# Seam between a ConvNeXt block's first convolution and its MLP: statistics of four images ahead, tiles three ahead, dummy TensorE passes

## The chip, the core and the metric

One Trainium2 chip, of which the kernel uses one core (TensorE, VectorE, ScalarE, GpSimd, and SyncE as a queue of transfers). The metric is the time of one execution on the device in microseconds (us), the median of several runs. In the profile the engines are called PE (TensorE), PEld (its weight loads), DVE (VectorE), ACT (ScalarE), POOL (GpSimd) and SP (SyncE).

## What is computed

x has 16 images of 96 channels of 56 x 56 points, in float32. Cut to what matters:

```python
y = depthwise_conv_7x7(x, dw_w) + dw_b                  # per channel
mu, var = mean_c(y), var_c(y)                           # over the 96 channels of a point
y = (y - mu) * rsqrt(var + 1e-6) * ln_w + ln_b
y = gelu(y @ w1 + b1)                                   # 96 -> 384
gx = sqrt(sum_over_points(y ** 2))                      # per image and hidden channel
nx = gx / (mean_hidden(gx) + 1e-6)
y = grn_gamma * (y * nx) + grn_beta + y
z = x + y @ w2 + b2                                     # 384 -> 96
out = depthwise_conv_3x3(floor_to_fixed(z), round_pow2(w)) + floor_to_fixed(bias)
```

## The kernel before, in words

Three stages follow each other, each with an instruction stream per engine that is written out by hand and tied by semaphores (`wait_ge`, `then_inc`; `need` is a wait that is dropped where its value is zero). No scheduler reorders anything: what an engine does next is what stands next in its block.

**First stage (7x7 convolution).** 96 channels in 24 batches of four (`CB`), all 16 images at once. PE turns rows (`tin`, L636), multiplies by banded tables (L664) and turns the result back (`back`, L686). ACT copies the results out (`yt_copy`, L803, and `out_copy`, L810), SP stores the convolved channels to `y_scratch` (L366). DVE keeps a running mean over the channels, and the running sum of squared deviations (`update`, L1017: the deviation L1021, the mean L1023, the weighted square L1025), POOL adds the squares up (`m2`, L557). In these arrays a column stands for points of one of the 16 images.

**Seam.** After channel 95: DVE makes the variance (L1031), ACT its root (L870, a table load and one pass), DVE the reciprocal with one Newton step (L1043 to L1047) and copies it into image order (`in_order`, L1038 to L1040). PE turns it to rows (L724, eight transposes), DVE copies the rows to SBUF (L1051), ACT stores them to `stats_scratch` (L872), waits until they have landed, and loads them back repeated over 96 partitions into `rb`: the first tile of image 0 (L876), the other six tiles of image 0 as one transfer (L877), image 1 (L878). SP first stores the tables of the last stage (`lines_c`, L407 to L409), waits for its stores, loads image 0 of y whole (L472), waits for `r_in[0]` (that is L877) and then loads image 1 of y whole, then seven tiles of x, and then images from 2 on by tiles (L478, L479).

**MLP.** An image is 7 tiles (`NCH`) of 448 points. For tile t of image i: DVE multiplies y by the factor of each point (`scale`, L1065) and rounds to the matmul's format (`high`, L1070), POOL makes the remainder (`low`, L568), PE multiplies by w1 in three parts and three groups of 128 hidden channels (`up`, L733 to L735: 9 matmuls), ACT applies gelu (L893). The squares of the hidden values are summed by ACT (L860), and of image 0 mostly by DVE (L1084); `part` 0 is the first four tiles, `part` 1 the last three, and m the group of hidden channels. Then DVE, POOL, PE and DVE make the GRN factors (`grn_sums` L1092, L577, the matmul with ones L758, `grn_scale` L1098 to L1109) that scale w2. PE's `down` (L743) multiplies by w2; ACT prepares x plus a constant (`with_constant`, L867), DVE adds and floors (L1117 to L1137), SP stores z (L488). The `steps` go over images: in step i, PE interleaves `up` of image i with `down` of image i-1, which runs `LEAD` = 2 tiles behind (in step 1 `FIRST_LEAD` = 3); DVE and POOL normalise tiles of image i+1, tile t in slot t, so seven tiles ahead. Step 0 is written out apart: DVE normalises image 0, tile 0 of image 1, sums squares, tile 1, more squares, the sums, tile 2.

**Last stage (3x3 convolution)** is built as the first; the change does not touch it, but for what it finds stored.

Of the kernel before, what the change touches and what calls it, by code (L numbers as in the profile page):

```python
# [35 lines left out]
HID = 4 * C  # L36
# [36 lines left out]
FIRST_LEAD = 3  # L73
# [21 lines left out]
def build(nc, x, dw_w, dw_b, ln_w, ln_b, w1, b1, grn_gamma, grn_beta, w2, b2, cw, cb, out):  # L95
# [8 lines left out]
    with ExitStack() as ctx:  # L104
# [72 lines left out]
        res1 = conv(IG * NPAIR, G * PAIR)  # L177
# [36 lines left out]
        p_stat = psum[:, 0:2, :]  # L214
# [32 lines left out]
        root_ready = sem("root_ready")  # L247
        stat_in = sem("stat_in")
# [3 lines left out]
        y_in = [sem("y_in0"), sem("y_in1")]  # L252
        x_in = [sem(f"x_in{t}") for t in range(NCH)]
        r_in = [sem("r_in0"), sem("r_in1")]
        r_first = sem("r_first")
# [52 lines left out]

        def rows_group(p, u):

            return ost[:, p, 2 * u:2 * u + 2, :].rearrange("p k (n r w) -> p (k n) r w", r=2, w=W)
# [39 lines left out]
        V_FIRST, V_LAST = MT + 1, 1  # L351

        def act_squares(i, m, part):
            if isinstance(i, int) and i == 0:
                return max(m - 1, 0)
            n = 2 * MT * i - V_FIRST + MT * part + m
# [32 lines left out]
        def _(sp):  # L389
# [35 lines left out]
            def conv_transfers(S, src, dst, tables):  # L425
# [36 lines left out]
            sp.wait_ge(lines_made, 2)  # L462
            store_lines(lines_c, lcb, zrow.bitcast(BF16)[:, 0:TW + LPAD], KC)


# [4 lines left out]
            def load_y(i, p):  # L470

                sp.dma_start(yraw[:, p, :], y_v[i]).then_inc(y_in[p], 16)  # L472

            def load_next(i, p, t):

                need(sp, scale_done, NCH * (i - 2) + t + 1)
                cols = slice(CH * t, CH * t + CH)
                sp.dma_start(yraw[:, p, cols], y_v[i][:, cols]).then_inc(t_in[p][t], 16)  # L478
                sp.dma_start(rb[:, p, cols], st_dram.ap().rearrange("(i o) t -> i o t", o=1)[i][:, cols].to_broadcast([C, CH])).then_inc(t_in[p][t], 16)  # L479
# [44 lines left out]
        def _(pool):  # L524
# [22 lines left out]
            def add(it, first, last):  # L547
                for k in range(2 * CB):
# [3 lines left out]
                    if not (last and p == 1):  # L552
                        for q in (AHEAD0 if first and p == 0 else AHEAD)[s]:
                            table_low(b + 1, q, 1 - p)
                    pool.wait_ge(wel, 3 * n + 3)
# [15 lines left out]
            def step(i, p):  # L571
                fixed = isinstance(i, int)
                for t in range(NCH):
# [4 lines left out]
                    if not (fixed and i >= NIMG - 1):  # L578
# [650 lines left out]
```

## Time and profile before

| | us |
|---|---|
| median of 3 runs (lowest, highest) | 1006.29 (1005.71, 1007.83) |
| the profiled execution: its own time | 1008.35 |
| its span, from first to last instruction | 1006.2 |
| busy in the span: PE / PEld | 939.4 / 694.5 |
| busy in the span: DVE / ACT / POOL | 806.6 / 756.5 / 415.7 |

A busy share is an average over three stages. The profile's chain of waits is followed back from the last instruction and says what released each step. The timeline lists the instructions of an engine with the idle time before each and what ended it. A table of stretches gives, for each stretch, the busy time of the engines and the clock that TensorE was granted (1.00 is 2.4 GHz, 0.50 is 1.2 GHz).

### The profile page before, as it was taken

Reading aid. Unit: us, or ns where it says so; the run is one execution under the profiler, and the core shown is the slowest. Engines: PE = TensorE matmul, PEld = TensorE weight load, DVE = VectorE, ACT = ScalarE, POOL = GpSimd, SP = SyncE. Lnnn points to the kernel's source line nnn. Section 1 sums busy time; section 2 is a strip of 40 time slices with the busy share of each in tenths; the row PEclk is TensorE's granted clock in tenths of the full one; section 3 lists DMA queues with packets and bytes.
Section 4 is the critical chain, followed back from the end, with each engine's and each line's share of the span. In section 5 each row is a group of like instructions: output and inputs, shape, how many; then the busy total and the mean of one; then the engine's idle time right before and its main releaser. Section 6 shows DMA issues by size and latency. Waiting matters only on the chain.

```text
span 1006.2 us, 22653 instructions
## 1 busy us (share of the span) xinstructions
PE 939.4 (93%) x6342; PEld 694.5 (69%) x6342; DVE 806.6 (80%) x1429; ACT 756.5 (75%) x1331; POOL 415.7 (41%) x357
## 2 busy tenths in 40 slices
PE   5799999999999179999999999999999985999997
PEld 4688888888888166666666666666666643877775
DVE  5688888888888487988888888888888785888876
ACT  3588888888887277789988888899888841666664
POOL 2577777777776164333332333323333100111110
PEclk9799999999999677999999999999999996999999
DMA  7566676777662592655555555555553235899996
GB/s 202 126 206 206 207 208 205 212 209 215 207 204 96 155 249 60 186 150 171 175 167 166 165 169 159 162 172 165 180 166 111 82 107 161 257 310 311 312 309 213
DMA packets 110260, 188.47 MB, mean 187 GB/s; under 512 B 17357, under 2 KB 104036, under 8 KB 107268
## 3 DMA queue, kind: packets, MB, share of 16 engines
q1 hardware_dynamic: 99988, 173.55, 57.9%
q10 hardware_dynamic: 10240, 14.53, 4.8%
q8 instruction: 15, 0.25, 0.1%
q14 instruction: 17, 0.14, 0.0%
HBM read 129.77 MB, written 58.25 MB: 187 GB/s over the span
## 4 chain that ended last, share of the span: by engine, by line
PE 76%; SPq 8%; DMA 5%; DVE 4%; issue 3%; ACT 2%; POOL 1%; ACTq 0%; DVEq 0%; POOLq 0%
PE psum L664 27%; PE psum L743 23%; PE psum L733 6%; PE psum L734 6%; PE psum L735 6%; SPq L371 4%; PE psum L686 4%; PE psum L636 3%; SPq L366 2%; SPq L383 1%; DMA arena_r<-y_scratch 1%; DMA arena<-lines_a 1%; ACT arena L860 1%; DMA arena<-z_scratch 1%; DMA arena_r<-stats_scratch 1%
## 5 line engine op out<-in xcount | busy, mean ns | idle before, releaser
L664 PE MATMUL psum<-arena_r 112*128 112x464 f32 x1536 | 362.1, 386 | 12.2 <-DVE arena_r L997 5.7
L664 PEld LDWEIGHTS psum<-arena_r 112*128 112x128 f32 x1536 | 285.6, 191 | 59.2 <-issue 10.1
L743 PE MATMUL psum<-arena,w2s 128*96 128x448 f32 x672 | 266.6, 541 | 2.8 <-DVE w2s L1109 2.8
L893 ACT ACTIVATE arena<-psum,b1g 128x448 f32<-128x448 f32 x336 | 202.4, 630 | 59.4 <-PE psum L735 59.4
L568 POOL TENSOR_TENSOR arena_r<-arena,arena_r 96x448 fp32r<-96x448 f32 x112 | 136.7, 1220 | 264.7 <-DVE arena_r L1070 238.5
L743 PEld LDWEIGHTS psum<-arena,w2s 128*96 128x96 f32 x672 | 109.8, 164 | 119.4 <-issue 112.0
L733 PE MATMUL psum<-arena_r,w1h 96*128 96x448 f32 x336 | 153.6, 457 | 14.9 <-POOL arena_r L568 14.9
L803 ACT ACTIVATE arena<-psum,bias_a 64x112 f32<-64x112 f32 (+1 forms) x288 | 107.6, 407 | 60.5 <-PE psum L664 58.9
L557 POOL TENSOR_TENSOR arena<-arena 128x448 f32<-128x448 f32 x96 | 111.2, 1158 | 84.0 <-DVE arena L1025 84.0
L791 ACT ACTIVATE arena_r<-psum 112x448 fp32r<-112x448 f32 x192 | 93.4, 541 | 61.5 <-PE psum L636 61.5
L860 ACT ACTIVATE arena<-arena 128x1792 bf16<-128x1792 f32 (+1 forms) x91 | 136.8, 1503 | 2.7
L542 POOL TENSOR_TENSOR arena_r<-arena,arena_r 112x512 fp32r<-112x512 f32 x96 | 122.8, 1291 | 16.6 <-ACT arena_r L818 16.6
L734 PE MATMUL psum<-arena_r,w1h 96*128 96x448 f32 x336 | 126.1, 375 | 0.0
L735 PE MATMUL psum<-arena_r,w1l 96*128 96x448 f32 x336 | 125.8, 374 | 0.0
L997 DVE TENSOR_TENSOR arena_r<-psum,arena_r 112x448 fp32r<-112x448 f32 x192 | 110.2, 615 | 13.2 <-ACT arena_r L791 13.1
L1021 DVE TENSOR_TENSOR arena<-arena,psum 128x448 f32<-128x448 f32 x96 | 59.3, 618 | 51.2 <-ACT arena L803 49.7
L1117 DVE TENSOR_TENSOR psum<-arena,psum 96x448 f32<-96x448 f32 x112 | 69.6, 622 | 32.3 <-PE psum L743 31.7
L733 PEld LDWEIGHTS psum<-arena_r,w1h 96*128 96x128 f32 x336 | 65.5, 195 | 36.8 <-POOL arena_r L568 16.7
L1025 DVE SCALAR_TENSOR_TENSOR arena<-arena,ck 128x448 f32<-128x448 f32 x96 | 88.9, 926 | 0.0
L599 POOL CAST arena_r<-arena 112x1024 fp32r<-112x1024 bf16 x24 | 25.0, 1043 | 148.1 <-PE psum L664 127.0
L867 ACT ACTIVATE arena<-arena,cvec 96x448 f32<-96x448 f32 x112 | 73.7, 661 | 11.1 <-DMA arena<-in_x_dram 7.2
L636 PE MATMUL psum<-ident,arena 64*112 64x64 f32 x1536 | 63.2, 225 | 18.5 <-DMA arena<-z_scratch 10.4
(100 smaller groups left out, 1043.1 us busy)
## 6 DMA issues: line engine op xcount, KB each, us to landing
arena<-in_x_dram SPq DMA_DIRECT2D x95, 224.0 KB, 5.0
arena<-lines_a SPq DMA_DIRECT2D x46, 448.0 KB
arena<-z_scratch SPq DMA_DIRECT2D x87, 224.0 KB, 4.7
y_scratch<-arena SPq DMA_DIRECT2D x96, 196.0 KB, 4.9
arena<-in_x_dram SPq DMA_DIRECT2D x112, 168.0 KB, 2.6
z_scratch<-arena SPq DMA_DIRECT2D x112, 168.0 KB, 2.0
arena_r<-y_scratch SPq DMA_DIRECT2D x98, 168.0 KB, 2.6
arena_r<-stats_scratch SPq DMA_DIRECT2D x98, 168.0 KB, 3.1
```

Of the source, the lines that this page charges most:

```text
L542: pool.tensor_tensor(toep_l[:, p, s, :], toep[:, p, s, :], toep_h[:, p, s, :].bitcast(F32), ALU.subtract).then_inc(A["tl"], 1)
L557: pool.tensor_tensor(m2, m2, dsq[:, k % 2, :], ALU.add).then_inc(m2_done, 1)
L568: pool.tensor_tensor(yl[:, CH * t:CH * t + CH], ct[:, (t + p) % 2, :], yh[:, CH * t:CH * t + CH].bitcast(F32), ALU.subtract).then_inc(yn_r ...
L664: mm = nc.tensor.matmul(p_conv[s % 2][:, 0:NCOL], w[:, p, s, TW * k:TW * k + TW], v[:, p, s, slot0 + k:slot0 + k + JP, :].rearrange("p j i ...
L733: nc.tensor.matmul(p_h[m][:, 0:CH], w1h[:, w], yh[:, cols], start=True, stop=False)
L734: nc.tensor.matmul(p_h[m][:, 0:CH], w1h[:, w], yl[:, cols], start=False, stop=False)
L735: nc.tensor.matmul(p_h[m][:, 0:CH], w1l[:, w], yh[:, cols], start=False, stop=True).then_inc(h_done, 1)
L743: mm = nc.tensor.matmul(p_o[k][0:C, 0:CH], w2s[:, p, m, :], hid[p][:, m, CH * t:CH * t + CH], start=(m == 0), stop=(m == MT - 1))
L803: ins = nc.scalar.activation(to, cols, ACT.Identity, bias=bias[part, bass.ds(n, 1)], scale=scale)
L860: nc.scalar.activation(sqd[:, 0:CH * (t1 - t0)], hid[p][:, m, CH * t0:CH * t1], ACT.Square, accum_out=ss[:, p, m, part:part + 1]).then_inc ...
L893: nc.scalar.activation(hid[p][:, m, CH * t:CH * t + CH], p_h[m][:, 0:CH], ACT.Gelu, bias=b1g[:, m:m + 1]).then_inc(gelu_done, 1)
L997: dve.tensor_tensor(turned(xt_l, p, u, half), in_bank(S, b, u, half), turned(xt_h, p, u, half).bitcast(F32), ALU.subtract).then_inc(S["xt" ...
```

## The change

On each engine's stream between the end of the first stage and step 2 of the MLP:

- **Statistics in two groups.** Images 0 to 3 (`of_images(v, 0, IG)`, a quarter of the columns) go through variance, root, reciprocal, reordering, turning, copying and storing first; the other twelve follow. DVE does the first group's reordering, ACT the second's, and ACT also copies the second group's rows from PSUM; SP stores them. The last channel's mean is no longer updated, and its square is made by DVE in `last_square`, which also adds it to `m2` in POOL's place.
- **Transposes.** The turned statistics lie in PSUM banks 6 and 7 in place of 0 and 1; the last `back` of the stage goes to banks 0 and 1, and no longer waits for the `out_copy` before it.
- **Tables of ACT.** A three-column Sqrt, and with it the table load, is put ahead of the last `yt_copy`; a three-column Gelu behind the second root.
- **Loads.** Images 0 and 1 are loaded by tiles, each tile with the semaphore `t_in`; `rb` of image 1 is loaded by SP. `lines_c` is stored in the first stage, after its first loop body.
- **Normalised tiles three ahead.** In slot t of step i DVE and POOL make tile t+3 of image i, and in slots 4 to 6 tiles 0 to 2 of image i+1 (`ahead_of`). `FIRST_LEAD` is gone: step 1 has `LEAD` = 2.
- **Squares of image 0.** The third group's part 0 goes from DVE to ACT.
- **Dummy passes.** PE multiplies w1h by itself into PSUM bank 2, 18 times before the first group's transposes and 32 times between them and the second's.

The diff, cut to its core:

```diff
+            def ahead_of(i, t):
+                return (i, t + 3) if t < NCH - 3 else (i + 1, t - (NCH - 3))
...
         def by_vector(i, m, part):
-            return isinstance(i, int) and (i == 0 and (part == 0 or m == 0) or i == NIMG - 1 and part == 1 and m == 0)
+            return isinstance(i, int) and (i == 0 and (m < 2 if part == 0 else m == 0) or i == NIMG - 1 and part == 1 and m == 0)
...
+                if S is stages["a"]:
+                    sp.wait_ge(lines_made, 2)
+                    store_lines(lines_c, lcb, zrow.bitcast(BF16)[:, 0:TW + LPAD], KC)
...
-            load_y(0, 0)
-            sp.wait_ge(r_in[0], 16)
-            load_y(1, 1)
+            for t in range(NCH):
+                load_y(0, 0, t)
+            sp.wait_ge(stat_out, 16)
+            for t in range(NCH):
+                load_y(1, 1, t)
+                load_r(1, 1, t)
             for t in range(NCH):
                 load_x(0, t)
+            sp.wait_ge(stat_rows, 2)
+            sp.dma_start(*stat_rows_of(1, G)).then_inc(stat_out, 16)
             for t in range(NCH):
                 load_next(2, 0, t)
+            sp.wait_ge(stat_out, 32)
...
# POOL, step
-                    if not (fixed and i >= NIMG - 1):
-                        low(i + 1, 1 - p, t)
+                    if fixed and i == 0:
+                        if t < 3:
+                            low(1, 1, t)
+                    elif not (fixed and (i == NIMG or i == NIMG - 1 and t >= NCH - 3)):
+                        j, u = ahead_of(i, t)
+                        low(j, p if t < NCH - 3 else 1 - p, u)
...
# PE
-                back(NBATCH - 1, 1, 1)
+                back(NBATCH - 1, 1, 1, psum[:, 0:2, :] if S is stages["a"] else None)
...
+            def keep_warm(passes):
+                for _ in range(passes):
+                    nc.tensor.matmul(bank[2][:, 0:HID], w1h[:, 0:128], w1h[:, :], start=True, stop=True)
...
+            pe.wait_ge(b1_made, 1)
+            keep_warm(WARM[0])
+            pe.wait_ge(stat_in, 1)
+            turn_stats(0, 1)
+            keep_warm(WARM[1])
+            pe.wait_ge(stat_in, 2)
+            turn_stats(1, G)
             pe.wait_ge(stages["a"]["out"], 2 * NBATCH)
...
# ACT
+                            if rows_too and last and p == 1 and s == CB - 1:
+                                nc.scalar.activation(gnx[:, :], halves[:, :], ACT.Sqrt)
...
                 if rows_too:
+                    act.wait_ge(var_ready, 1)
+                    nc.scalar.activation(of_images(root, 0, IG), of_images(var, 0, IG), ACT.Sqrt).then_inc(root_ready, 1)
                     out_copy(NBATCH - 1, 1, 1)
...
             act.wait_ge(stat_rows, 1)
+            act.dma_start(*stat_rows_of(0, 1)).then_inc(stat_out, 16)
+            act.wait_ge(var_ready, 2)
+            nc.scalar.activation(of_images(root, IG, NIMG), of_images(var, IG, NIMG), ACT.Sqrt).then_inc(root_ready, 1)
+            nc.scalar.activation(gnx[:, :], halves[:, :], ACT.Gelu)
             act.wait_ge(stat_out, 16)
+            for t in range(NCH):
+                act.dma_start(rb[:, 0, CH * t:CH * t + CH], r_tile(0, t)).then_inc(t_in[0][t], 16)
+            act.wait_ge(rstd_made, 1)
+            for to, v in in_order(IG, NIMG):
+                ins = nc.scalar.activation(to, v, ACT.Identity)
+            ins.then_inc(stat_in, 1)
+            act.wait_ge(stat_t, 2)
+            nc.scalar.activation(*stat_images(1, G), ACT.Identity).then_inc(stat_rows, 1)
...
# DVE
+            dve.wait_ge(m2_done, C - 1)
+            last_square(0, IG)
+            dve.wait_ge(root_ready, 1)
+            link(one_over(0, IG))
+            for to, v in in_order(0, IG):
+                ins = dve.tensor_copy(to, v)
+            ins.then_inc(stat_in, 1)
+            last_square(IG, NIMG)
+            dve.wait_ge(stat_t, 1)
+            dve.tensor_copy(*stat_images(0, 1)).then_inc(stat_rows, 1)
+            dve.wait_ge(root_ready, 2)
+            one_over(IG, NIMG).then_inc(rstd_made, 1)
...
-                    for m in range(MT):
-                        squares(0, 0, m, 0)
+                    squares(0, 0, 0, 0)
+                    squares(0, 0, 1, 0)
                     normalise(1, 1, 1)
...
                     grn_scale(0, 0)
-                    for t in range(3, NCH):
-                        normalise(1, 1, t)
...
-                        if norm and ahead:
-                            norm(i + 1, 1 - p, t)
+                        if norm and ahead and not (fixed and i == NIMG - 1 and t >= NCH - 3):
+                            j, u = ahead_of(i, t)
+                            norm(j, p if t < NCH - 3 else 1 - p, u)
```

How the streams stand at three places (line, operation, output <- inputs, shape, count; line numbers of either kernel's own file).

TensorE, from the last transposes of the first stage to the first `up`; L686 in the kernel before and L733 in the changed one are `back`. Before:

```order
L664 MATMUL psum<-arena_r 128x464 x24
L686 MATMUL psum<-ident,arena 112x56 x32
L724 MATMUL psum<-ident,arena 112x56 x8
L733 MATMUL psum<-arena_r,w1h 128x448
L734 MATMUL psum<-arena_r,w1h 128x448
```

and now:

```order
L709 MATMUL psum<-arena_r 128x464 x24
L733 MATMUL psum<-ident,arena 112x56 x32
L769 MATMUL psum<-w1h 128x384 x18
L776 MATMUL psum<-ident,arena 112x56 x2
L769 MATMUL psum<-w1h 128x384 x32
L776 MATMUL psum<-ident,arena 112x56 x6
L794 MATMUL psum<-arena_r,w1h 128x448
L795 MATMUL psum<-arena_r,w1h 128x448
```

The eight statistics transposes have become two and six, with the dummy passes before each part; the six stand ahead of the first `up`.

ScalarE, from the last `yt_copy` to the first gelu (L803, L863 are `yt_copy`, L810, L871 `out_copy`, L893, L962 gelu). Before:

```order
L803 ACTIVATE arena<-psum,bias_a 128x336
L803 ACTIVATE arena<-psum,bias_a 64x112 x2
L810 ACTIVATE arena<-psum 112x896 x2
L870 ACT_TABLE_LOAD
L870 ACTIVATE arena<-arena 128x448
L872 DMA stats_scratch<-arena 112x4x112
L876 DMA arena_r<-stats_scratch 96x448
L877 DMA arena_r<-stats_scratch 96x2688
L878 DMA arena_r<-stats_scratch 96x3136
L893 ACT_TABLE_LOAD
L893 ACTIVATE arena<-psum,b1g 128x448 x21
```

and now:

```order
L900 ACT_TABLE_LOAD
L900 ACTIVATE gnx<-halves 128x3
L863 ACTIVATE arena<-psum,bias_a 128x336
L863 ACTIVATE arena<-psum,bias_a 64x112 x2
L871 ACTIVATE arena<-psum 112x896
L910 ACTIVATE arena<-arena 128x4x28
L871 ACTIVATE arena<-psum 112x896
L935 DMA stats_scratch<-arena 112x112
L937 ACTIVATE arena<-arena 128x4x84
L938 ACT_TABLE_LOAD
L938 ACTIVATE gnx<-halves 128x3
L941 DMA arena_r<-stats_scratch 96x448 x7
```

The root of the first group stands between the two `out_copy`; the first table load stands ahead of the last `yt_copy`, the second ahead of the loads of `rb`.

VectorE, from the last tile of image 0 in step 0 to the GRN sums (L1065, L1133 are `scale`, L1070, L1138 `high`, L1084, L1152 squares). Before:

```order
L1084 SCALAR_TENSOR_TENSOR arena,ss<-arena 128x1792 x3
L1065 TENSOR_TENSOR arena<-arena_r 96x448
L1070 CAST arena_r<-arena 96x448
L1084 SCALAR_TENSOR_TENSOR arena,ss<-arena 128x1344
L1092 TENSOR_REDUCE ss<-ss 128x3
```

and now:

```order
L1152 SCALAR_TENSOR_TENSOR arena,ss<-arena 128x1792 x2
L1133 TENSOR_TENSOR arena<-arena_r 96x448
L1138 CAST arena_r<-arena 96x448
L1152 SCALAR_TENSOR_TENSOR arena,ss<-arena 128x1344
L1160 TENSOR_REDUCE ss<-ss 128x3
```

One of the three wide squares ahead of tile 1 of image 1 is gone from this engine.

## Rows read from the trace of the kernel before

**Rows 1.** Stretches: us, busy and count by engine, granted clock, DMA share, GB/s.

```profile
356.00:360.50 4.50, 4.50 (x12) 4.07 (x13) 4.40 (x7) 1.90 (x3) 3.62 (x3) 0.50 0.97 227
361.00:371.00 10.00, 10.00 (x50) 9.04 (x49) 8.97 (x10) 9.98 (x16) 5.74 (x4) 1.00 1.02 266
500.00:760.00 260.00, 260.00 (x963) 168.92 (x962) 219.82 (x457) 229.88 (x360) 85.77 (x72) 1.00 0.56 167
819.00:822.00 3.00, 3.00 (x6) 1.09 (x5) 1.83 (x3) 0.67 (x1) 0.00 (x0) 0.57 0.16 48
```

**Rows 2.** Chain of waits around the seam: start, us, what.

```profile
333.05 1.28 ACT L870
...
334.95 2.96 DVE arena L1043
...
341.90 0.64 PE psum L724 x8
...
343.21 2.43 DMA stats_scratch<-arena
...
346.04 7.27 DMA arena_r<-stats_scratch
353.32 10.70 DMA arena_r<-y_scratch
```

**Rows 3.** Timeline of PE: start, us, engine, line, what, count, [idle before <- releaser].

```profile
331.43 0.64 PE L686 MATMUL psum<-ident,arena 56*112 56x56 f32 x16 [1.68 <-ACT arena L810]
...
351.49 0.74 PE L733 MATMUL psum<-arena_r,w1h 96*128 96x448 f32 x1 [8.97 <-POOL arena_r L568]
...
375.88 0.74 PE L733 MATMUL psum<-arena_r,w1h 96*128 96x448 f32 x1 [4.52 <-POOL arena_r L568]
...
384.06 0.74 PE L733 MATMUL psum<-arena_r,w1h 96*128 96x448 f32 x1 [0.67 <-POOL arena_r L568]
...
789.35 0.41 PE L733 MATMUL psum<-arena_r,w1h 96*128 96x448 f32 x1
...
818.45 16.80 PE L743 MATMUL psum<-arena,w2s 128*96 128x448 f32 x40 [2.78 <-DVE w2s L1109]
```

**Rows 4.** Timeline of DVE, first tiles, squares, and a later image's sums.

```profile
349.12 0.62 DVE L1065 TENSOR_TENSOR arena<-arena_r 96x448 f32<-96x448 f32 x1 [5.94 <-DMA arena_r<-stats_scratch]
...
354.94 1.21 DVE L1070 CAST arena_r<-arena 96x448 fp32r<-96x448 f32 x1
...
365.34 2.02 DVE L1084 SCALAR_TENSOR_TENSOR arena<-arena 128x1792 f32<-128x1792 f32 x1
...
367.47 2.79 DVE L1084 SCALAR_TENSOR_TENSOR arena<-arena 128x1792 f32<-128x1792 f32 x1
...
785.59 0.16 DVE L1092 TENSOR_REDUCE ss<-ss 128x3 f32<-128x6 f32 x1 [1.71 <-ACT arena L860]
```

**Rows 5.** Timeline of ACT: copies, gelus, squares, x plus constant.

```profile
329.21 1.14 ACT L803 ACTIVATE arena<-psum,bias_a 128x336 f32<-128x336 f32 x3 [1.39 <-PE psum L664]
...
360.83 9.34 ACT L893 ACTIVATE arena<-psum,b1g 128x448 f32<-128x448 f32 x15 [0.49 <-PE psum L735]
370.08 1.31 ACT L860 ACTIVATE arena<-arena 128x1344 bf16<-128x1344 f32 x1
...
372.90 0.65 ACT L867 ACTIVATE arena<-arena,cvec 96x448 f32<-96x448 f32 x1
...
392.63 1.69 ACT L860 ACTIVATE arena<-arena 128x1792 bf16<-128x1792 f32 x1
```

**Rows 6.** Timeline of POOL: remainders of three tiles.

```profile
350.31 1.12 POOL L568 TENSOR_TENSOR arena_r<-arena,arena_r 96x448 fp32r<-96x448 f32 x1 [16.79 <-DVE arena_r L1070]
...
373.45 2.38 POOL L568 TENSOR_TENSOR arena_r<-arena,arena_r 96x448 fp32r<-96x448 f32 x1 [5.07 <-DVE arena_r L1070]
...
787.29 1.15 POOL L568 TENSOR_TENSOR arena_r<-arena,arena_r 96x448 fp32r<-96x448 f32 x1
```

**Rows 7.** Waits of SP's queue at the seam: us, times, longest.

```profile
SPq L468 <- DMA lines_c<-arena: 1.3, 1, 1.3
```

More of the change, by code:

```diff
@@ L554, in add @@
                             table_low(b + 1, q, 1 - p)
+                    if last and k == 2 * CB - 1:
+                        return
                     pool.wait_ge(wel, 3 * n + 3)
@@ L675, in back_waits, with back @@
                     evicted(pe, S, b, 2 * u + 1)
-                    need(pe, S["out"], 2 * b + u + 1 - len(outs))
-                def back(b, u, p):
+                    if not (S is stages["a"] and isinstance(b, int) and (b, u) == (NBATCH - 1, 1)):
+                        need(pe, S["out"], 2 * b + u + 1 - len(outs))
+                def back(b, u, p, to=None):
+                    to = outs[u % len(outs)] if to is None else to
                     for k in range(2):
@@ L749, in step @@
                 head, tail = fixed and i == 0, fixed and i == NIMG
-                lead = FIRST_LEAD if fixed and i == 1 else LEAD
-                for t in range(NCH + lead):
+                for t in range(NCH + LEAD):
                     if t < NCH and not tail:
@@ L758, in step @@
                         nc.tensor.matmul(p_grn[1 - p], ones[:, :], gx[:, :], start=True, stop=True).then_inc(gsum_done, 1)
-                    if t >= lead and not head:
-                        down(i - 1, 1 - p, t - lead)
+                    if t >= LEAD and not head:
+                        down(i - 1, 1 - p, t - LEAD)
             steps(pe, step)
@@ L1022, in update @@
                 dve.wait_ge(wel, 3 * n + 1)
+                if isinstance(b, int) and n == C - 1:
+                    return
                 dve.scalar_tensor_tensor(out=mean, in0=dev, scalar=rk[:, bass.ds(n, 1)], in1=mean, op0=ALU.mult, op1=ALU.add).then_inc(wel, 1)
@@ L1042, in _, with last_square @@
-            dve.wait_ge(root_ready, 1)
-            link(dve.reciprocal(rstd, root))
-            link(dve.tensor_tensor(dsq[:, 0, :], rstd, rstd, ALU.mult))
-            link(dve.tensor_tensor(dsq[:, 0, :], dsq[:, 0, :], var, ALU.mult))
-            link(dve.tensor_scalar(dsq[:, 0, :], dsq[:, 0, :], -0.5, 1.5, ALU.mult, ALU.add))
-            link(dve.tensor_tensor(rstd, rstd, dsq[:, 0, :], ALU.mult))
-            in_order(rstd_in, rstd).then_inc(stat_in, 1)
+            def last_square(n0, n1):
+                part = [of_images(v, n0, n1) for v in (dsq[:, 0, :], dev, m2, var)]
+                link(dve.scalar_tensor_tensor(out=part[0], in0=part[1], scalar=ck[:, C - 1:C], in1=part[1], op0=ALU.mult, op1=ALU.mult))
+                link(dve.tensor_tensor(part[2], part[2], part[0], ALU.add))
+                dve.tensor_scalar(part[3], part[2], 1.0 / C, LN_EPS, ALU.mult, ALU.add).then_inc(var_ready, 1)
@@ new lines, in one_over @@
+            def one_over(n0, n1):
+                r, q, v, to = [of_images(v, n0, n1) for v in (root, dsq[:, 0, :], var, rstd)]
+                link(dve.reciprocal(to, r))
+                link(dve.tensor_tensor(q, to, to, ALU.mult))
+                link(dve.tensor_tensor(q, q, v, ALU.mult))
+                link(dve.tensor_scalar(q, q, -0.5, 1.5, ALU.mult, ALU.add))
+                return dve.tensor_tensor(to, to, q, ALU.mult)
+            dve.wait_ge(m2_done, C - 1)
+            last_square(0, IG)
@@ L1142, in step @@
                 head, tail = fixed and i == 0, fixed and i == NIMG
-                ahead = not (fixed and i >= NIMG - 1)
+                ahead = not (fixed and i == NIMG)
                 if head:
```

94 lines of the change are left out of this document (41 added, 53 removed).

## Prediction

> **What bounds the kernel now.** The stretches first [rows 1]: through the MLP PE is busy all the time at the full clock, so inside the MLP only PE's own work counts, and DVE (85% busy there) and ACT (88%) have room. The chain of waits next [rows 2], to see where PE does not set the pace: between the first stage and the MLP it runs over DVE, one ACT table load, the eight transposes and three transfers in a row. PE's timeline says the same as idle time [rows 3]: the first `up` begins at 351.49 after 8.97 us idle, the tile (1,1) (tile 1 of image 1) at 375.88 after 4.52 us idle. Both times PE comes back at half clock (the first row of [rows 1]): 12 matmuls in 4.50 us, 0.37 us each, against 0.21 at full clock (15 gelus, one per three matmuls, in 9.34 us [rows 5], so 1.87 us a tile).
>
> The sum has four terms: when the first `up` starts, how long it takes to tile (1,1), what follows up to step 2, and the rest of the MLP. It is made against the profiled execution (1008.35 us, of which 1006.2 are span). That one lies 0.2% above the median of 1006.29, so I carry the difference over to the median. A measurement of this kernel can tell about 0.2% (2 us) from no change.
>
> **First `up`, 351.49 before.** The last `yt_copy` ends at 329.21 + 1.14 = 330.35 [rows 5]. DVE's deviation (0.6) ends at 331.0. `last_square` on a quarter of the columns: three instructions, 0.9, to 331.9. ACT's root of a quarter, 0.4, to 332.3. Then DVE has eight instructions. On all columns they took from 334.95 to the transposes at 341.90 [rows 2], 6.95 us; a quarter is 1.7, and a three-column instruction still takes 0.16 [rows 4], so the floor of eight adds about 1. I take 2.7 (ends: 1.7 and 6.9, far nearer the quarter, since the columns are a quarter): 335.0. Two of eight transposes, 0.4: 335.4. DVE has begun the other images' squares meanwhile (1.5), then copies the rows: 336.8. Storing them costs 2.43 as now [rows 2]: 339.2. On ACT the second root (0.5) and the Gelu load (1.28 [rows 2]) lie beside that transfer. The first tile of `rb`, issued at 345.67 and used at 349.12 [rows 4], took 3.45: 342.7. From there to PE is as now, 351.49 - 349.12 = 2.37: **first `up` at 345.1, -6.4 us**.
>
> What must fit beside it: y of image 0 is issued from 336.9, or 0.4 earlier, as SP no longer waits 1.3 us for `lines_c` [rows 7]; that store moves to a place early in the first stage where SP waits for the next batch anyway, and costs nothing. The second group: root done at 338.0, DVE's five instructions on three quarters of the columns (4.1) to 342.1, ACT's seven transfer issues until 342.5 and its three copies (1.1) to 343.6, six transposes (0.5) to 344.2. These stand ahead of the first `up` in PE's queue, and have 0.9 us to spare. The 32 dummy passes start at 335.4 and at full clock take 32 x 0.21 x 384/448 = 5.7 us, so they end at 341.1, also in time.
>
> The Sqrt load stands ahead of the last `yt_copy`, in an idle time of 1.39 us [rows 5]. Its row shows 1.28 [rows 2], and ACT computes directly behind it; with the three-column pass the copy slips by 0.1, which I drop. The Trainium skill (ScalarE: Activation LUTs, "What ACT_TABLE_LOAD costs") says that a drain of about 1.38 us comes on top of each load; by that page the last `yt_copy` would slip by 1.3 us and the first `up` with it, to 346.4. The trace has no such drain behind the load at 333.05.
>
> **From the first `up` to tile (1,1): 24.4 us before.** Seven tiles at full clock are 7 x 1.87 = 13.1. The clock will probably be low at the start again, though for less: PE idles from 341.1 to about 343.6 where it idled 8.97. The nearest row is the idle time of 2.78 us in the tail [rows 3], behind which the clock was at 0.57 for three microseconds (the last row of [rows 1]): three slow microseconds and a bit, a cost of 1.7. Ends: 0 (clock kept), and 3.5, what the low stretch costs now (21 matmuls from 351.49 to 360.6, each 0.165 slower). The last gelu ends 0.7 behind its matmul: 345.1 + 13.1 + 1.7 + 0.7 = 360.6. Then ACT's squares of image 0, one wide (1.69 + 0.19 for reading the sum) and two narrow (1.31 + 0.19 each) [rows 5], 4.9; then x plus constant, 0.65, and the first gelu of tile (1,0), 0.55, which frees the bank that (1,1) needs: **366.7**. The other way in is DVE: eight tiles 1.78 us apart (0.62, and a cast that takes 1.21 beside POOL, less a little overlap [rows 4]), to 356.9, two wide squares (2.02 to 2.79 each [rows 4], 4.8) to 361.7, tile (1,1) at 362.7, POOL's remainder in its slow form, 2.38 [rows 6], to 365.1. So ACT, to which a square was moved, is now last by 1.6 us; before, it was POOL. 21.6 us in place of 24.4: **-2.8**. Data are there in time: `rb` of image 0 must bring a tile per 1.78 us, and the larger transfer now brings six in 7.27 [rows 2], 1.2 each; y of image 1, which arrived only 10.7 us after `rb` of image 0 [rows 2] since SP held it back, is now issued from 340.
>
> **From tile (1,1) to step 2.** The same six `up` and seven `down`. PE idles 4.9 us ahead of it, 4.5 before, so I expect the low clock again, as long as now. What goes is the 0.67 us wait of tile (1,3) [rows 3]: now the first `down` stands between (1,2) and (1,3), and covers DVE's `grn_scale` and POOL. **-0.7**.
>
> **The rest.** An image is 107 matmul records (63 of `up`, 42 of `down`, 2 of the GRN); with 963 in 260 us [rows 1] it takes PE 28.9 us at the full clock, without a wait; normalising three instead of seven tiles ahead gives PE nothing. It costs nothing as long as the third tile of the next image is there: its remainder is the one POOL makes behind the GRN root, ending at 787.29 + 1.15 = 788.44 [rows 6], and PE would want it at 789.35 [rows 3], 0.9 us later. Step 15 now normalises four tiles, in slots in which earlier steps did so without delaying PE. 0.
>
> Sum: -6.4 - 2.8 - 0.7 = **-9.9 us**: 998.45 for an execution like the profiled one, **996.4** for the median.
>
> **Rivals.**
> 1. *PE keeps the full clock at both places.* For it: the dummy passes, and the first gap is a third of the old one. Against: the gap ahead of (1,1) has no dummy passes, and one like it (4.52) ended in low clock. The first place gives 1.7 more, and at the second three `up` of nine matmuls now run 0.165 slower each, 4.5: 996.4 - 6.2 = 990.2.
> 2. *The first `up` comes later than worked out.* Should the dummy passes run at half clock, they take 10.2 us, to 345.6, the six transposes come behind them, and the first `up` at 346.3 (+1.2), with 3.5 of slow clock in place of 1.7: 999.4. Should the small tiles of `rb` land as late as the large transfer (7.27 in place of 3.45), it is +3.8: 1000.2. With the two in part together, about 1000.5, at worst 1003. For it: y and `rb` of two images now compete on the same DMA engines.
> 3. *Slower: the third tile is late in every image.* A wait of PE on POOL's remainder of tile (i+1, 2), right behind the GRN root. It decides above 0.9 us of delay and would recur in 14 images; from 1.6 us on it eats the whole gain; at 1.9, 14 us are lost: 1010.4. Against: ACT's squares, DVE's sums [rows 4] and POOL's root keep their times, and only the tile in that slot changes its number.
> 4. *The change does not do what it says:* the gain at the first `up` is spent in waiting ahead of (1,1), for instance by ACT for x of image 0, which now stands behind 28 tile transfers. At 96 x 448 float32 values each they are 4.8 MB; at 266 GB/s [rows 1] from 336.9 that is until 355, and x is wanted at 365. It would have to be ten microseconds later still. Then 1006.
> 5. *The Sqrt load costs about twice its row in its new place.* Then 2.6 us stand in 1.39 idle, and the last `yt_copy` and all behind it slip by 1.2: 997.6. Against: ACT's pass directly behind the load at 333.05. The page of the Trainium skill named above stands behind this rival.
>
> **How the numbers follow.** Forecast 58% (996.4, its own range 993 to 999.5 by the two ends of the slow clock and half a microsecond on each transfer); rival 1 14%; rival 2 14%; rival 5 5%; rival 4 5%; rival 3 4%. The 80% range runs from 990 to 1002: it takes in rivals 1, 2 and 5 and leaves out 3 and 4 and the far tails. Faster by over 0.2%: all but rivals 3, 4: 91%. Within 0.2%: 5%. Slower: 4%.
>
> **What would show it.** In the changed profile: the Sqrt load inside the idle time ahead of the last `yt_copy`; the store of rows at about 336.8; the first `scale` near 342.7 and the first `up` near 345; a short stretch at half clock; ACT's squares ending near 365.5 and (1,1) at 366.7, released by ACT and not by POOL; 28.9 us an image afterwards. I am wrong if the first `up` comes after 348, if (1,1) waits for a transfer, or if a steady image takes more than 29 us.

## The result, and the profile after

The changed kernel takes **1041.95 us** (median of 4 runs, 1041.16 to 1043.71) against 1006.45 before (1005.71 to 1007.83): a ratio of 1.0353, 95% interval 1.0336 to 1.0371. It is 35.5 us slower; 996.4 was forecast, with a range of 990 to 1002. The profiled execution took 1043.71 us, of which 1041.9 are span.

The stretches of the changed kernel, as in [rows 1] (us, then busy and count of PE, PEld, DVE, ACT and POOL, granted clock, DMA share, GB/s): the two half-clock places of the seam, then three steps of the MLP, each from one image's GRN matmul to the next image's, and a piece of 3.3 us inside the second of these.

```profile
345.30:351.90 6.60, 4.46 (x17) 3.89 (x18) 6.01 (x8) 1.92 (x4) 3.89 (x3) 0.51 1.07 271
369.00:379.00 10.00, 9.81 (x24) 7.62 (x25) 3.17 (x12) 6.56 (x12) 3.10 (x3) 0.50 0.33 81
402.86:434.13 31.27, 29.25 (x108) 18.73 (x108) 24.62 (x52) 25.66 (x41) 9.74 (x9) 1.00 0.52 155
434.13:467.21 33.08, 30.93 (x108) 19.49 (x108) 24.53 (x52) 25.70 (x41) 9.45 (x9) 0.95 0.49 146
467.21:498.69 31.48, 29.23 (x109) 18.79 (x108) 24.55 (x52) 25.63 (x41) 9.56 (x9) 1.00 0.54 154
444.10:447.40 3.30, 3.30 (x7) 1.76 (x6) 1.15 (x2) 1.99 (x4) 0.06 (x1) 0.50 0.39 115
```

The same step in the kernel before:

```profile
439.96:468.91 28.95, 28.95 (x107) 18.86 (x107) 24.30 (x52) 25.55 (x41) 9.38 (x8) 1.00 0.55 164
```

The number of matmuls is the same (one record more or less at an edge), and the busy times of DVE, ACT and POOL differ by under 0.4 us. What has changed is that PE is no longer busy throughout: 31.27 - 29.25 = 2.02 us idle in the first of the three steps. The second costs 1.8 more, 0.1 of it a longer wait, the rest because 3.3 us of it ran at half clock. Where the idle time stands, the waits of PE over the whole run say (us in total, times, longest):

```profile
PE psum L794 <- POOL arena_r L609: 32.9, 15, 2.3
...
PE psum L794 <- ACT arena L962: 4.6, 1, 4.6
PE psum L776 <- ACT arena L944: 3.9, 1, 3.9
```

Fifteen waits of an `up` for POOL's remainder (L609), at most 2.3 each: one at the first `up` (2.1), and 30.8 in 14 steps, one in each. The two waits for ACT belong to the seam. PE's timeline shows the seam's places, as in [rows 3] (start, us, engine, line, operation, operands, count, idle before and who ended it), and the new wait in two steps:

```profile
345.34 0.53 PE L776 MATMUL psum<-ident,arena 56*112 56x56 f32 x6 [3.87 <-ACT arena L944]
347.96 0.71 PE L794 MATMUL psum<-arena_r,w1h 96*128 96x448 f32 x1 [2.10 <-POOL arena_r L609]
...
369.19 0.71 PE L794 MATMUL psum<-arena_r,w1h 96*128 96x448 f32 x1 [4.60 <-ACT arena L962]
...
406.79 2.42 PE L804 MATMUL psum<-arena,w2s 128*96 128x448 f32 x6
411.23 0.47 PE L794 MATMUL psum<-arena_r,w1h 96*128 96x448 f32 x1 [2.02 <-POOL arena_r L609]
411.53 0.36 PE L795 MATMUL psum<-arena_r,w1h 96*128 96x448 f32 x1
...
442.72 0.46 PE L794 MATMUL psum<-arena_r,w1h 96*128 96x448 f32 x1 [2.15 <-POOL arena_r L609]
...
444.07 0.57 PE L794 MATMUL psum<-arena_r,w1h 96*128 96x448 f32 x1
...
445.19 3.52 PE L804 MATMUL psum<-arena,w2s 128*96 128x448 f32 x6
```

The seam did get shorter: first `up` at 347.96 (351.49 before), tile (1,1) at 369.19 (375.88 before), tile (2,0) at 400.58 (408.76 before). That is -8.2 us by step 2. From there on every step waits at one place: behind the `down` of tile (i-1, 0), PE wants the `up` of tile (i, 3) and does not have it. What DVE and POOL did in those microseconds of step 2 (DVE's timeline, then POOL's):

```profile
404.54 0.15 DVE L1166 TENSOR_REDUCE gsum<-psum 128x1 f32<-128x3 f32 x1
...
405.56 0.63 DVE L1177 TENSOR_SCALAR w2s<-w2r,gsc 128x96 f32<-128x96 f32 x3
406.11 0.62 DVE L1185 TENSOR_TENSOR psum<-arena,psum 96x448 f32<-96x448 f32 x1
...
408.08 0.62 DVE L1205 SCALAR_TENSOR_TENSOR arena<-psum,arena 96x448 f32<-96x448 f32 x1
408.62 0.61 DVE L1133 TENSOR_TENSOR arena<-arena_r 96x448 f32<-96x448 f32 x1
409.26 0.39 DVE L1138 CAST arena_r<-arena 96x448 fp32r<-96x448 f32 x1
```

```profile
402.84 1.15 POOL L609 TENSOR_TENSOR arena_r<-arena,arena_r 96x448 fp32r<-96x448 f32 x1
409.73 1.44 POOL L609 TENSOR_TENSOR arena_r<-arena,arena_r 96x448 fp32r<-96x448 f32 x1 [5.74 <-DVE arena_r L1138]
```

At the start of step 2, DVE reads in this order: the GRN scale of image 1 (to 406.1), the four instructions that floor tile 6 of image 0 (L1185 to L1205, to 408.6), and only then the scale of tile (2,3) (L1133), its cast, and POOL's remainder (to 411.2). PE's `down` of tile (1,0) had ended at 409.2. POOL sat idle for 5.74 us, waiting for DVE, so it is not POOL that is slow. The remainder at 402.84 is tile (2,2), the one whose slack the prediction had worked out; it ended at 403.99, for an `up` at 404.99, and was in time. The one after it was not.

**The books.** The 14 steps from the GRN matmul at 402.86 to the one at 851.80 take 448.9 us, 32.07 each. Before, the same 14, from 410.95 to 815.28, took 404.3, 28.88 each: +44.6. Of these 30.8 are the waits. Six of the steps hold a half-clock stretch such as 444.1 to 447.4 (granted clock 0.95 over the step, 1.00 in the others); they take 33.11 on average, the other steps 31.43 without the last one, so about 1.7 each, 10.2. The last 3.6 are what is left, 0.26 a step. I take them for the price of stopping and restarting: from the start of the `down` to the second matmul of the `up` it takes 4.74 us here (406.79 to 411.53), and 2.45 in run 3 below, where nothing waits (405.43 to 407.88), which is 0.27 more than the 2.02 of the wait. With -8.1 at the seam and -0.8 behind the last GRN, +44.6 gives +35.7, the difference of the two spans.

In the shares of the chain that ended last, PE's has fallen by 17 points, and DVE, ACT and what counts as issue stand in its place; first the kernel before, then the changed one:

```profile
PE 76%; SPq 8%; DMA 5%; DVE 4%; issue 3%; ACT 2%; POOL 1%; ACTq 0%; DVEq 0%; POOLq 0%
```

```profile
PE 59%; DVE 10%; issue 10%; ACT 8%; DMA 4%; SPq 4%; POOL 2%; DVEq 0%; POOLq 0%; ACTq 0%
```

### The profile page after: what moved, and what is told of

The parts are those of the page before. It is cut to its first block, busy times and chain, and to the rows that moved or that the text cites. A ratio compares the mean times of both kernels' runs of the same rounds, so it can differ in the third digit from the quotient of the medians.

```text
span 1041.9 us, 22771 instructions
## 1 busy us (share of the span) xinstructions
PE 960.7 (92%) x6392; PEld 704.6 (68%) x6392; DVE 802.4 (77%) x1435; ACT 761.3 (73%) x1340; POOL 414.3 (40%) x356
## 4 chain that ended last, share of the span: by engine, by line
PE 59%; DVE 10%; issue 10%; ACT 8%; DMA 4%; SPq 4%; POOL 2%; DVEq 0%; POOLq 0%; ACTq 0%
PE psum L709 28%; PE psum L804 12%; ACT arena L925 5%; PE psum L733 4%; PE psum L794 4%; PE psum L796 4%; PE psum L795 4%; PE psum L681 3%; SPq L402 2%; POOL arena_r L609 2%; ACT arena L962 2%; DVE psum L1197 2%; DVE arena L1191 2%; DVE psum L1185 1%; DMA z_scratch<-arena 1%
## 5 line engine op out<-in xcount | busy, mean ns | idle before, releaser
L804 PE MATMUL psum<-arena,w2s 128*96 128x448 f32 x672 | 277.4, 559 | 2.8 <-DVE w2s L1177 2.8
L962 ACT ACTIVATE arena<-psum,b1g 128x448 f32<-128x448 f32 x336 | 202.6, 631 | 98.2 <-PE psum L796 97.9
L609 POOL TENSOR_TENSOR arena_r<-arena,arena_r 96x448 fp32r<-96x448 f32 x112 | 136.3, 1217 | 316.9 <-DVE arena_r L1138 315.3
L804 PEld LDWEIGHTS psum<-arena,w2s 128*96 128x96 f32 x672 | 113.9, 170 | 126.3 <-issue 118.6
L794 PE MATMUL psum<-arena_r,w1h 96*128 96x448 f32 x336 | 149.1, 444 | 37.5 <-POOL arena_r L609 32.9
L863 ACT ACTIVATE arena<-psum,bias_a 64x112 f32<-64x112 f32 (+1 forms) x288 | 107.8, 408 | 59.0 <-PE psum L709 57.2
L925 ACT ACTIVATE arena<-arena 128x1344 bf16<-128x1344 f32 (+1 forms) x92 | 138.5, 1505 | 2.8
L1185 DVE TENSOR_TENSOR psum<-arena,psum 96x448 f32<-96x448 f32 x112 | 69.7, 622 | 77.5 <-PE psum L804 77.4
L795 PE MATMUL psum<-arena_r,w1h 96*128 96x448 f32 x336 | 125.2, 373 | 0.0
```

The costliest lines, as they stand in the source:

```text
L609: pool.tensor_tensor(yl[:, CH * t:CH * t + CH], ct[:, (t + p) % 2, :], yh[:, CH * t:CH * t + CH].bitcast(F32), ALU.subtract).then_inc(yn_r ...
L794: nc.tensor.matmul(p_h[m][:, 0:CH], w1h[:, w], yh[:, cols], start=True, stop=False)
L795: nc.tensor.matmul(p_h[m][:, 0:CH], w1h[:, w], yl[:, cols], start=False, stop=False)
L804: mm = nc.tensor.matmul(p_o[k][0:C, 0:CH], w2s[:, p, m, :], hid[p][:, m, CH * t:CH * t + CH], start=(m == 0), stop=(m == MT - 1))
L863: ins = nc.scalar.activation(to, cols, ACT.Identity, bias=bias[part, bass.ds(n, 1)], scale=scale)
L925: nc.scalar.activation(sqd[:, 0:CH * (t1 - t0)], hid[p][:, m, CH * t0:CH * t1], ACT.Square, accum_out=ss[:, p, m, part:part + 1]).then_inc ...
```

## The experiments

**Theory 1: the fourth tile is late.** In each step tile (i,3) is normalised behind `grn_scale` and the flooring of an older tile on DVE, where PE needs it within three `up` and one `down`. The seam's gain is real. **Rivals:** the new seam itself disturbs the steady images (clock, or transfers out of step); or POOL or the cast has become slower beside other work.

**1. Seven ahead again, with the new seam.** All images are normalised a whole image ahead, as in the kernel before; the new statistics, loads and dummy passes stay.

```
-                        if norm and ahead and not (...):
-                            j, u = ahead_of(i, t)
-                            norm(j, p if t < NCH - 3 else 1 - p, u)
+                        if norm and ahead:
+                            norm(i + 1, 1 - p, t)
```

(POOL's side likewise; tiles 3 to 6 of image 1 are normalised in step 1 ahead of its slots, and `FIRST_LEAD = 3` is back.)

> The changed kernel, but DVE and POOL normalise seven tiles ahead again and step 1 has its lead of three. Theory 1 (late tile 3: in slot 0 DVE makes the GRN factors and floors the last tile of image i-2 before it normalises tile (i,3), which PE wants 5.8 us after the GRN matmul): the wait of PE of 2.0 to 2.3 us at the fourth tile goes from every image, an image takes 28.9 us instead of 31.3 to 33.1, and 8 us of gain from the seam stay: about 998 us. Theory 2 (the seam itself leaves PE in a worse state, through the dummy passes or the loads by tiles, and the images pay for it): about 1042, with images of 31 to 33 us as in the changed kernel.

Measured: 999.4 us (998.08 to 1000.82) against 1006.23, ratio 0.9927 (0.9904 to 0.9951). An image takes 28.97 us (steps 2 to 14 on average; 28.95 in the kernel before), and no wait at tile 3 is left. So the new seam with the old look-ahead is 7 us faster than before, and all of the loss is in normalising three ahead. Of these 7, its trace has 4.7 at the GRN matmul of image 1 (406.25 against 410.95) and 2.8 behind the last one, in a stretch that the change does not touch.

**2. Three ahead alone, with the old seam.** The other half of the change, put into the kernel before.

```
-                        if norm and ahead:
-                            norm(i + 1, 1 - p, t)
+                        if norm and ahead and not (...):
+                            j, u = ahead_of(i, t)
+                            norm(j, p if t < NCH - 3 else 1 - p, u)
```

> The kernel before with nothing but the three-ahead normalising. Theory 1: the wait of 2.2 us at tile 3 of images 2 to 15 appears and drags short stretches at half clock behind it: 44 us slower, about 1050 us. Theory 2: no change, 1006 us.

Measured: 1057.71 us (1055.78 to 1059.27), ratio 1.0505 (1.0477 to 1.0533): the loss comes without the new seam, and the rival that the seam disturbs the images falls. It is 7 us more than expected. Three waits of the same kind stand in step 1 as well, since this kernel keeps its first lead of three tiles; the step takes 42.5 us in place of 31.6, at a mean granted clock of 0.81 (PE's timeline):

```profile
392.88 0.47 PE L741 MATMUL psum<-arena_r,w1h 96*128 96x448 f32 x1 [2.22 <-POOL arena_r L572]
399.46 0.48 PE L741 MATMUL psum<-arena_r,w1h 96*128 96x448 f32 x1 [2.21 <-POOL arena_r L572]
406.04 0.74 PE L741 MATMUL psum<-arena_r,w1h 96*128 96x448 f32 x1 [2.22 <-POOL arena_r L572]
```

**3. The tile first, then the flooring.** The changed kernel, with one piece of DVE's program moved: from step 2 on the normalising of (i,3) stands behind `grn_scale` but ahead of the flooring of tile 6 of image i-2. Number and kind of all instructions are the same.

```
+                    if not tail:
+                        for stage in (scale, high):
+                            stage(i, p, 3)
...
-                        if norm and ahead and not (...):
+                        if norm and ahead and not (...) and (t > 0 or fixed and i == 1):
```

> The changed kernel with one move on DVE: tile (i,3) is normalised before the last tile of image i-2 is floored, not after it. Theory 1: the tile is ready about 2.6 us sooner, at the moment when PE wants it, so no wait or one of at most 0.3 us is left: 998 to 1003 us, images of 28.9 us. Theory 1b (POOL's remainder and the cast, not DVE's place in line, make the tile late): the wait shrinks by less than a micro-second, 1025 or more. Theory 2: 1042.

Measured: 995.81 us (994.86 to 996.17), ratio 0.9893 (0.9871 to 0.9914), 28.93 us an image. Step 2 again, DVE, then POOL, then PE:

```profile
404.74 0.61 DVE L1133 TENSOR_TENSOR arena<-arena_r 96x448 f32<-96x448 f32 x1
405.39 0.39 DVE L1138 CAST arena_r<-arena 96x448 fp32r<-96x448 f32 x1
405.70 0.62 DVE L1185 TENSOR_TENSOR psum<-arena,psum 96x448 f32<-96x448 f32 x1
```

```profile
405.86 1.13 POOL L609 TENSOR_TENSOR arena_r<-arena,arena_r 96x448 fp32r<-96x448 f32 x1 [3.24 <-DVE arena_r L1138]
```

```profile
405.43 2.42 PE L804 MATMUL psum<-arena,w2s 128*96 128x448 f32 x6
407.33 0.71 PE L794 MATMUL psum<-arena_r,w1h 96*128 96x448 f32 x1
407.88 0.37 PE L795 MATMUL psum<-arena_r,w1h 96*128 96x448 f32 x1
```

The tile is ready at 405.86 + 1.13 = 406.99, and its `up` begins at 407.33. The margin is 0.3 us. With the same work on DVE and POOL, 2.6 us of place in DVE's order decide 46 us of the kernel. POOL's instruction takes 1.13 here and 1.44 in the changed kernel; 0.3 us could not have caused a wait of 2.0, so the second rival falls too. The kernel came out 2 us below the range expected (998 to 1003): in its trace the first `up` is 1.9 sooner than in the changed kernel (346.06 against 347.96) and the part behind the last GRN matmul 1.3 shorter (188.8 against 190.1), and the edit touches neither.

**4. Four ahead.** The changed kernel with `t + 4` in place of `t + 3` in `ahead_of` and its bounds; tile (1,3) is normalised ahead of step 1's slots.

```
-            return (i, t + 3) if t < NCH - 3 else (i + 1, t - (NCH - 3))
+            return (i, t + 4) if t < NCH - 4 else (i + 1, t - (NCH - 4))
```

> The changed kernel with tiles normalised four ahead: tile 3 of image i+1 is made in slot 6 of step i, tile (i,4) in slot 0. Theory 1: PE wants (i,4) 4.1 us after (i,3), which is more than the 2.5 us by which it was late: no wait, 28.9 us an image, 998 us. Theory 2: 1042.

Measured: 994.46 us (994.16 to 997.18), ratio 0.9882 (0.986 to 0.9903), 28.93 us an image, no wait at tile 3. One tile more of look-ahead changes +35.5 us into -12; 998 was expected, and the first `up` is again sooner (346.55) than in the changed kernel, for no reason that the edit gives. The following runs start from this kernel (in the texts of the expectations it goes by its label), and take the seam apart. It was itself measured on another chip and not again beside them, and its four times run from 994.16 to 997.18, so a difference of 2 to 3 us between its median and theirs shows little by itself, and the traces have to be read beside the medians. With four ahead the first `up` stands at 346.55, tile (1,1) at 368.41, the GRN matmul of image 0 at 371.90 and that of image 1 at 402.43.

**5. Without the dummy passes.** `WARM = (18, 32)` becomes `(0, 0)`. PE's results are the same; the passes write a bank that is overwritten.

> e4_four_ahead without the 18 and 32 dummy passes. If they hold TensorE's clock: half clock from about 345 to about 360 in place of 345 to 352, 1.5 to 3.5 us slower than e4_four_ahead (996 to 998). If the clock at the first tiles does not depend on them: the same 994.5.

Measured: 997.0 us (995.1 to 997.67), ratio 0.9903 (0.9888 to 0.9918). The stretches, first of this kernel, then of the one with four ahead (columns as above):

```profile
333.20:353.50 20.30, 7.80 (x27) 6.75 (x28) 15.21 (x24) 7.17 (x12) 6.22 (x5) 0.50 0.91 234
```

```profile
345.00:352.00 7.00, 5.95 (x21) 5.23 (x22) 5.90 (x9) 2.95 (x5) 5.08 (x4) 0.52 1.07 259
365.60:379.30 13.70, 10.89 (x27) 7.93 (x27) 5.81 (x16) 9.08 (x16) 6.03 (x5) 0.51 0.45 118
```

Without the passes the clock is at half for 20.3 us, with them for under 7; but most of the 20.3 us lie ahead of the first `up`, where PE has little to do. The first `up` is at 346.58 in one and 346.55 in the other. The GRN matmul of image 0 comes 0.9 us later without the passes (372.78), that of image 1 no later (402.09 against 402.43): behind the gap ahead of tile (1,1), PE works at half clock from 369.3 to 377.5 in one, from 368.4 to 379.1 in the other, which gives the 0.9 back. So the traces show a gain of 0.9 us at the first tiles, and nothing of it at step 2. The medians differ by 2.5 us, but their intervals overlap, and that the passes are worth it is not shown.

**6. Image 0's tiles alone on the queues.** SP issues image 1's loads only when the first tile of `rb` of image 0 has landed.

```
-            sp.wait_ge(stat_out, 16)
+            sp.wait_ge(t_in[0][0], 32)
```

> e4_four_ahead, but SP issues the loads of image 1 only when the first tile of image 0's factors has landed. If the loads of image 1 beside it are why that tile took 5.7 us to land and not 3.45: the first tile of the MLP starts up to 1 us sooner (the second group's transposes hold it from 345.5 on), about 993.5. If its time is its own: no change at the first tile, and at most a loss further on.

Measured: 996.87 us (995.87 to 999.11), ratio 0.991 (0.9897 to 0.9924). The first tile, issued at 340.08, is used at 344.98, after 4.90 us; with four ahead it was 339.03 to 344.09, 5.06. Holding back image 1's loads gains nothing (993.5 was expected if they were the reason). The median is 2.4 us above that with four ahead, though the tile was issued 1.05 us later before the edit could act: such offsets stand between executions of the same code. What else delays the tile (the loads of y of image 0 share the DMA engines) was not tried alone and stays open.

**7. Dummy passes in the gap ahead of tile (1,1).** 24 passes into another bank between the `up` of (1,0) and that of (1,1), where the changed kernel idles 4.6 us and comes back at half clock.

```
+                    if fixed and i == 1 and t == 1:
+                        keep_warm(24, bank[6])
```

> e4_four_ahead with 24 more dummy passes between the first and second tile of image 1, where TensorE idles 4.8 us. If the idle time there is what drops the clock: no low stretch of 13.7 us behind it, three tiles at 1.9 in place of 3.4 us, 4 us sooner (990.5). If the clock falls all the same: 994.5, or more where the passes hold the tile up.

Measured: **992.34 us** (991.21 to 994.6), ratio 0.9866 (0.9851 to 0.9881), the fastest of all. PE's timeline and a stretch of this kernel, then the same stretch with four ahead:

```profile
365.62 4.34 PE L769 MATMUL psum<-w1h 96*128 96x384 f32 x24
370.51 0.44 PE L794 MATMUL psum<-arena_r,w1h 96*128 96x448 f32 x1 [0.56 <-ACT arena L964]
```

```profile
368.00:378.00 10.00, 9.44 (x43) 7.19 (x42) 6.17 (x17) 8.37 (x16) 4.61 (x4) 1.00 0.36 95
```

```profile
368.00:378.00 10.00, 9.59 (x24) 7.40 (x25) 5.10 (x15) 6.77 (x12) 4.47 (x4) 0.50 0.36 95
```

The same ten microseconds hold 43 matmuls in place of 24. From the GRN matmul of image 0 to that of image 1 it takes 27.4 us (372.39 to 399.82) in place of 30.5. By the medians it is 2.1 us against four ahead, with intervals that overlap (990.5 was expected), and 4.5 to 4.7 against runs 5, 6 and 8, with intervals that do not.

**8. The third wide square back on DVE.** Undoes the part of the change that gave ACT one square of image 0 more (DVE's call and the counts of the squares likewise).

```
-            return isinstance(i, int) and (i == 0 and (m < 2 if part == 0 else m == 0) ...)
+            return isinstance(i, int) and (i == 0 and (part == 0 or m == 0) ...)
```

> e4_four_ahead with the third wide square of image 0 back on DVE. Theory: ACT is last ahead of tile (1,1), by 1.4 us before DVE and POOL; with the square back DVE is later by 2.8 us and becomes last, the tile starts about 1.4 us later: 995.9. Rival: the squares lie off the path, no change.

Measured: 996.92 us (996.18 to 999.01), ratio 0.9917 (0.9904 to 0.9931). Tile (1,1), at 368.41 behind ACT with four ahead, comes at 369.17 behind POOL. So it is POOL, behind DVE, that is last again, as expected:

```profile
369.17 0.74 PE L794 MATMUL psum<-arena_r,w1h 96*128 96x448 f32 x1 [3.83 <-POOL arena_r L609]
```

What the square's move is worth this does not show. By the medians the kernel is 2.5 us slower, and the intervals just miss each other; but the first `up` was late too, at 347.53, and from there to tile (1,1) it takes 21.6 us, with four ahead 21.9. The GRN matmul of image 1 comes at 402.05, 0.4 sooner than with four ahead, and the profiled execution is the shorter one (996.18 against 997.18).

**9. The statistics of all 16 images in one group.** Four ahead, dummy passes as long as the new gap.

> e4_four_ahead with the statistics of all 16 images in one group (and 54 first dummy passes, to fill the longer time). Theory: the split is the seam's gain, since three quarters of squares, reciprocal and copies (0.85 + 4.3 us), of the transposes and of the row copy (0.6) come back onto the path ahead of the first tile: first up at about 352, 5 to 6 us slower than e4_four_ahead, 1000. Rival: the loads by tiles and the table loads are the gain; then less than 2 us are lost.

Measured: 999.94 us (999.17 to 1001.98), ratio 0.9933 (0.9912 to 0.9954); the first `up` at 350.84. Splitting the statistics is worth about 5.5 us by the medians and 4.3 at the first `up` by the traces (350.84 against 346.55), the largest part of the seam's gain.

**10. Four ahead alone, with the old seam.**

> The kernel before with four tiles ahead, and a lead of two in step 1 as in all steps; its old seam is kept. Theory: in the steady images nothing changes (28.9 us each), in step 1 PE no longer waits 0.67 us for tile (1,3) and meets less half clock: 0.5 to 2 us faster than before, 1004.5 to 1006. Rival: four ahead costs in the old seam too, above 1008.

Measured: 1003.53 us (1001.98 to 1006.32), ratio 0.9971 (0.9957 to 0.9985), 28.97 us an image. A shorter look-ahead with enough slack costs nothing in the steps, and gains 2.3 us in step 1 (GRN of image 0 to GRN of image 1: 29.3 us, 31.6 before), a little more than expected.

## Why the prediction was wrong

**The step that failed is "The rest", counted as 0.** It said: "It costs nothing as long as the third tile of the next image is there", and found 0.9 us of slack for it. That condition was needed and was met: POOL's remainder of tile (2,2) ran at 402.84, in time. But it was not the only one. With three ahead the tile (i,3) is normalised in the first slot of step i itself, and its slack was never worked out. All its prices were to be had: DVE's chain takes 5.1 us from the GRN sums on (404.54 to 409.65: the scale of image i-1, a flooring of 2.6, a scale and a cast), then POOL's remainder, 1.1 to 1.4, while PE has only what is left of two tiles' `up` and one `down` (404.54 to 409.2 here). 404.54 to 411.17 is 6.6 us, against 4.7: that is the wait of 2.0. The sentence on step 15, "in slots in which earlier steps did so without delaying PE", shows the error of thought: in the kernel before, a tile normalised in slot 0 was needed 29 us later, so its delay could not show. Runs 3 and 4 show the cause: with the tile moved ahead of the flooring, or made a slot earlier, the wait is gone.

**Rival 3** named the right kind of mechanism (a wait of PE on POOL's remainder that recurs in 14 images) but the wrong tile, and so reasons against it that did not bear on the real one; its 4% was far too little. Its price, 14 us, was for a tile 1.9 us late with 0.9 of slack, so 1.0 us of wait an image. The waits measured 2.2 us on average, and it had no term for what came with them: 0.26 each of restart, and in six of 14 a half-clock stretch that cost 1.7.

**The seam**, by its own steps:

- *First `up`*: 347.96, not 345.1; -3.5, not -6.4. The work up to the store was right: rows stored at 337.10 (336.8 forecast), tiles issued at 339.76 (339.2). What was mis-sized is the landing of the first tile of `rb`: the first `scale` comes at 345.51, 5.75 us behind its issue, where 3.45 was taken; nearer the upper end of rival 2 than the forecast. DVE's row and ACT's for this place:

```profile
345.51 0.62 DVE L1133 TENSOR_TENSOR arena<-arena_r 96x448 f32<-96x448 f32 x1 [3.23 <-DMA arena_r<-stats_scratch]
```

```profile
328.12 1.28 ACT L900 ACT_TABLE_LOAD   x1
329.41 0.21 ACT L900 ACTIVATE gnx<-halves 128x3 f32<-128x3 f32 x1
329.63 1.14 ACT L863 ACTIVATE arena<-psum,bias_a 128x336 f32<-128x336 f32 x3
...
339.76 3.88 ACTq L941 DMA_DIRECT2D arena_r<-stats_scratch  x7
343.69 1.60 ACT L944 ACTIVATE arena<-arena 64x336 f32<-64x336 f32 x3 [4.18 <-issue]
...
363.18 1.69 ACT L925 ACTIVATE arena<-arena 128x1792 bf16<-128x1792 f32 x1
```

- *Rival 5 falls*: the Sqrt load ends at 329.40 and the next pass begins at 329.41; the last `yt_copy` slipped by some 0.4 (329.63, 329.21 before), of which 0.3 stood already ahead of the load. The Trainium skill (ScalarE: Activation LUTs, "What ACT_TABLE_LOAD costs") gives a load of about 1283 ns and a drain of about 1380 ns. This trace agrees with the first and shows nothing of the second, neither here, where the pass ahead of the load ends at 328.10 and the load begins at 328.12, nor at the Gelu load (338.01 + 1.28, next pass at 339.30); the sum goes by the measurement.
- *The second group's turn*: 345.34, not 343.7. ACT could start its three copies only at 343.69, behind seven transfer issues of 3.88 us in all, and they took 1.60, not 1.1. It still came before POOL released the first `up`.
- *Half clock at the start*: right. It lasted from 345.3 to 351.9, 10 matmuls of the `up` ran at 0.37 us in place of 0.20, 1.7 us, as forecast, though PE had idled longer than the 2.5 us that the forecast took: 3.87 ahead of the transposes and 2.10 behind them. That the size came out the same is in part luck.
- *To tile (1,1)*: right. 21.2 us from the first `up` (21.6 forecast), released by ACT and not POOL, as forecast; ACT's squares began at 363.18, and run 8 shows POOL last again once ACT has one less. -3.2 in place of -2.8. But run 8, with the old squares, takes 21.6 us here as well, so the square's move is not what brought the gain.
- *To step 2*: -1.5 in place of -0.7. The 0.67 us wait of tile (1,3) is gone as forecast; beyond it, half clock lasts from 369.2 to 379.1, 9.9 us, and not as long as before, when it went from 375.9 to 388.0.

In sum the seam gave -8.2 where -9.9 was forecast. The versions in which no tile is late (999.4, 995.8, 994.5) stand around the forecast of 996.4, in part by luck. In their traces the GRN matmul of image 1 comes 4.7, 9.5 and 8.5 us sooner than before, and a further 2.8, 2.2 and 2.0 us lie behind the last GRN matmul, where the prediction counted nothing: 190.9 us before, in an execution 2 us above its median, and 188.1 to 188.9 in these. What differs there was not tried.

## What to carry to other kernels

When a change shortens how far a producer runs ahead, list for every slot what stands before it on its in-order engine and when the consumer wants it; the slots at a step's start, where one-off work (here the GRN scale) and leftovers of an older image queue up, decide, and checking one tile is not checking the next. Room in an engine's busy share (77% on DVE) says nothing about this: one `up` tile more of look-ahead, or moving the urgent tile ahead of a flooring that nobody waits for, was worth 46 us or more. If PE must idle at a known place, dummy passes into a free bank can hold its clock; whether that saves time shows only once the next stretches are read too (run 5 against run 7).

## What was not expected of the hardware

- A wait of 2.0 to 2.3 us in an otherwise busy PE was followed by half clock for about 3.3 us in six of 14 steps, and not in the other eight: after the 2.15 us idle ahead of 442.72 the matmuls ran at full clock until 444.07, then at half until 447.4. On average over the 14 steps the idle time counts once and a half for that (44.6 us for 30.8 of wait). The wait of 2.02 ahead of 411.23 brought none. What decides which of them do was not settled.
- 24 passes of 96x384, 4.34 us, in an idle time of 4.8 us kept the full clock (run 7), where without them it was low from 365.6 to 379.1.
- The first 168 KB tile of `rb` took 4.9 to 5.75 us from issue to use, against 3.45 before. Between issue and use the DMA share was 0.84 in the changed kernel (339.76 to 345.51) and 0.62 before (345.67 to 349.12). That the busier queues are the cause is not shown: holding back the second image's loads left 4.90 at a share of 0.82 (run 6).
